# Decoder block on one core: attention values moved to head-major rows by small transfers, and divided there

## The reference

```
x = layernorm(x + selfattention(x))        # low-rank q and kv (128), rotary part, 1024 keys, softmax, @ Wo + bo
x = layernorm(x + crossattention(x, ctx))  # 154 keys, mask, softmax, @ W3.T + b3
x = layernorm(x + moe(x))                  # 8 experts, each takes its 256 best tokens, silu MLP 256-512-256
```

## Time and profile before

| what | before |
|---|---|
| time of three runs | 1958.56, 1962.59 (median), 1962.68 us |
| the profiled execution | 1959.72 us |
| its span, first to last instruction | 1957.9 us |
| mean granted PE clock | 0.907 of full speed |
| busy: PE, DVE, ACT, POOL | 85%, 58%, 46%, 22% of the span |

### The profile page before, as it was taken

The page is one execution under the profiler, slowest core; times in us unless marked ns, Lnnn a source line. Parts: engine busy times, 40 slices in busy tenths (PEclk is TensorE's granted clock), DMA queues, the critical chain, the costliest instruction groups (busy, mean ns, idle before and its releaser), DMA issues. The chain is left out here.

```text
span 1957.9 us, 32981 instructions
## 1 busy us (share of the span) xinstructions
PE 1668.1 (85%) x10632; PEld 848.3 (43%) x10632; DVE 1134.5 (58%) x1939; ACT 891.8 (46%) x1585; POOL 429.8 (22%) x547
## 2 busy tenths in 40 slices
PE   6599988798999888989998798999967844999993
PEld 3033334444332445433324354333245433888883
DVE  5577725756777256567763665677435366333424
ACT  2077773342777534347774343577833300111112
POOL 5200004302000052020001611100031001555563
PEclk9599999897999988979998899799988955999997
DMA  6700003622000044220000632200003040335446
GB/s 187 163 2 1 2 25 87 163 48 71 2 2 2 27 127 134 49 59 2 2 2 27 164 98 53 54 2 2 2 21 78 2 150 28 75 77 107 77 89 193
DMA packets 98037, 120.07 MB, mean 61 GB/s; under 512 B 17180, under 2 KB 73500, under 8 KB 97820
## 3 DMA queue, kind: packets, MB, share of 16 engines
q1 hardware_dynamic: 85468, 97.13, 18.1%
q0 software_dynamic: 12416, 20.98, 5.7%
HBM read 80.30 MB, written 40.79 MB: 62 GB/s over the span
## 5 line engine op out<-in xcount | busy, mean ns | idle before, releaser
L881 ACT ACTIVATE pT<-banks 128x512 f32<-128x512 f32 x1184 | 645.2, 596 | 254.8 <-PE banks L1492 150.0
L1034 DVE TENSOR_REDUCE nmf<-banks 128x1 f32<-128x1024 f32 x512 | 606.0, 1220 | 173.5 <-PE banks L1442 171.6
L1492 PE MATMUL banks<-qst,kst 99*128 99x512 bf16 x1024 | 344.0, 388 | 12.1 <-DVE nmf L1034 6.3
L1442 PE MATMUL banks<-kst,qst 96*128 96x512 bf16 x1024 | 327.0, 404 | 31.9 <-DMA kst<-k_parts 21.8
L1524 PE MATMUL banks<-pT,V 128*32 128x512 f32 x2048 | 273.8, 606 | 20.6 <-ACT oT L872 14.0
L1492 PEld LDWEIGHTS banks<-qst,kst 99*128 99x128 bf16 x1024 | 96.0, 97 | 307.2 <-ACT pT L881 185.8
L703 POOL CAST nmp<-nmf 128x16 bf16<-128x16 f32 x64 | 12.7, 198 | 831.4 <-DVE nmf L1034 516.6
L944 ACT ACTIVATE kst<-banks 128x512 f32<-128x512 f32 x64 | 38.2, 597 | 287.0 <-PE banks L1747 278.6
L1442 PEld LDWEIGHTS banks<-kst,qst 96*128 96x128 bf16 x1024 | 98.6, 100 | 146.4 <-DVE nmf L1034 37.3
L1029 DVE TENSOR_REDUCE nmf<-banks 128x4 f32<-128x616 f32 x128 | 99.6, 797 | 86.6 <-PE banks L1436 79.7
L1053 DVE RECIPROCAL rz<-banks 128x16 f32<-128x16 f32 x64 | 16.1, 251 | 204.5 <-PE banks L1552 203.4
(11 more groups left out here) (176 smaller groups left out, 2016.7 us busy)
## 6 DMA issues: line engine op xcount, KB each, us to landing
qst<-q_parts SPq DMA_DIRECT2D x48, 256.0 KB, 5.2
kst<-k_parts SPq DMA_DIRECT2D x48, 256.0 KB, 3.8
qst<-in_w SPq DMA_DIRECT2D x16, 512.0 KB
q_parts<-kst SPq DMA_DIRECT2D x48, 128.0 KB, 2.5
k_parts<-kst SPq DMA_DIRECT2D x48, 128.0 KB, 3.9
qx_parts<-kst SPq DMA_DIRECT2D x48, 128.0 KB, 3.1
qxs<-qx_parts SPq DMA_DIRECT2D x24, 256.0 KB, 5.0
qst<-qx_parts SPq DMA_DIRECT2D x24, 256.0 KB, 4.9
```

What stands on the lines that cost most here:

```text
L881: act.activation(pT[:, n % RING_P, :], PS[:, banks[what, n], :], ACT.Exp, scale=scale).then_inc(s_ex, 1)
L1034: dve.tensor_reduce(nmf[:, m % 2, j, t:t + 1], scores.rearrange("p a n -> p (a n)"), AX.X, ALU.max, negate=True).then_inc(s_smu, 1)
L1442: ins = pe.matmul(pair[:, half, :], qst[0:KQ, h, t * P:(t + 1) * P], kst[0:KQ, h, half * N:(half + 1) * N], start=True, stop=True)
L1492: ins = pe.matmul(ps, kst[0:KM, head, kc * P:(kc + 1) * P], qst[0:KM, head, cols], start=True, stop=True)
```

## The change

`empty` copies the bank into one of two slots `avr[:, group % 2, :]`. When it has done so, SP issues five DMAs for the group (`compact`): one takes the four rows of sums to 4 partitions of `sums` (32 x 512 when all are there: 2 x head + half), four take 16 rows of 2 KB each to the rows of the head in `xT`. In self-attention `compact(g - 2)` stands behind `load_minus_max(g)`, the last two behind `load_x(b + 1)`; in cross-attention `compact(g - 4)`, the last four behind `load_ones`. ACT waits for the transfers of group g - 2 before it fills a slot. In the junction DVE (`divided`) waits for all transfers and inverts `sums` in one instruction, 32 partitions x 512. PE (`inverses`) spreads the inverses over the rows of the heads with four float32 matmuls (32 rows of the operand `spread` of zeros and ones, 512 columns), and DVE multiplies them into `xT` with 4 instructions of 128 x 512. `output` follows, and takes a half as soon as its two multiplications are done. `o_tiles`, `turn_tokens` and the copies of the junction are gone.

The order changes with it: `latents` (b+1) stand ahead of `inverses` and `output`, `context_values` (b+1) too, on PE and on DVE; POOL's `split` of the context's keys stands ahead of the second `rsqrt`. `xTf`, `mask_i` have rooms of their own, `load_x` waits for the first st instead of the last, and ACT's wait for the mask goes. POOL makes `spread` once with a memset and four selects.

```diff
-EACH = Plan(OUT_SELF + LATENTS + INTO_CROSS + OPERANDS, OUT_CROSS + CONTEXT + ROUTING)
+EACH = Plan(LATENTS + OUT_SELF + INTO_CROSS + OPERANDS, CONTEXT + OUT_CROSS + ROUTING)
...
+            def compact(b, cross, g):
+
+                wait_apart(sp, s_ave, b * 2 * NG + (NG if cross else 0) + g + 1)
+                slot = avr[:, g % 2, :]
+                sp.dma_start(sums[TILES * g:TILES * (g + 1), :], slot[HD:P:V32, :]).then_inc(s_oc[g % 2], 16)
+                for j in range(TILES):
+                    (h, half), rows = (g * G + j // HALVES, j % HALVES), slice(V32 * j, V32 * j + HD)
+                    sp.dma_start(xT[h % 8 * HD:(h % 8 + 1) * HD, h // 8, half * N:(half + 1) * N],
+                                 slot[rows, :]).then_inc(s_oc[g % 2], 16)
...
             def self_attention(b):
                 for g in range(NG):
                     load_minus_max(b, g, qst[:, g * G:(g + 1) * G, :])
+                    if g >= 2:
+                        compact(b, False, g - 2)
...
                     load_minus_max(b, NG + g, cross_rows(g))
+                    if g >= 4:
+                        compact(b, True, g - 4)
                 if more:
                     load_ones()
+                for g in range(NG - 4, NG):
+                    compact(b, True, g)
...
-                    if n0 == 0 and k == 0:
-
-                        act.wait_ge(s_mask, b + 1 + START)
-                    act.activation(oT[:, k, :], PS[:, AV_BANK, :], ACT.Copy).then_inc(s_ave, 1)
+
+                    act.wait_ge(s_oc[k % 2], 80 * (b * NG + (NG // 2 if n0 else 0) + k // 2) + START)
+                    act.activation(avr[:, k % 2, :], PS[:, AV_BANK, :], ACT.Copy).then_inc(s_ave, 1)
...
+            def divided(at, b, name, cross):
+
+                for i in range(2):
+                    dve.wait_ge(s_oc[i], 80 * (b * NG + (NG if cross else NG // 2)) + START)
+                dve.reciprocal(sums[:, :], sums[:, :]).then_inc(s_rz, 1)
+                for n in range(4):
+                    idx, (half, c) = at.nth(name, n), divmod(n, 2)
+                    cols = slice(half * N, (half + 1) * N)
                     ready(at, idx)
...
+                    dve.tensor_tensor(xT[:, c, cols], xT[:, c, cols], PS[:, at.bank(idx), :],
+                                      ALU.mult).then_inc(s_evd, 1)
...
+            def inverses(at, b, name, cross):
+
+                pe.wait_ge(s_rz, b * 2 + (2 if cross else 1))
+                for n in range(4):
+                    half, c = divmod(n, 2)
+                    pe.matmul(item(at, at.nth(name, n)), spread[:, c, half, :], sums[:, :],
+                              start=True, stop=True).then_inc(s_item, 1)
 
             def output(at, t_name, y_name, w):
-                taken_upto(at, at.nth(t_name, 3) + 1)
                 for k in range(4):
+                    taken_upto(at, at.nth(t_name, k // 2 * 2 + 1) + 1)
...
-                o_tiles(at, "o", 0, T)
-                turn_heads(at, "o", "oT")
-                output(at, "oT", "y", wo)
                 if more:
                     latents(at, b + 1)
+                inverses(at, b, "bc", False)
+                output(at, "bc", "y", wo)
...
-                o_tiles(at, "ox", 0, T)
-                turn_heads(at, "ox", "oxT")
-                output(at, "oxT", "yx", w3)
                 if more:
                     context_values(at)
+                inverses(at, b, "bcx", True)
+                output(at, "bcx", "yx", w3)
```

More of the change, by code:

```diff
@@ L251, in decoder_block @@
         mhalf = sb("mhalf", [P, T])
-        oT = sb("oT", [P, NG, N])
-        early = oT[:, :, :].rearrange("p g n -> p (g n)")
-        mask_i = early[:, 0:T * SK].bitcast(I32).rearrange("p (t k) -> p t k", k=SK)
+        avr = sb("avr", [P, 2, N])
+        mask_i = sb("mask_i", [P, T, SK], I32)
+        sums = sb("sums", [H * HALVES, N])
+        spread = sb("spread", [H * HALVES, C, HALVES, P])
+        xTf = sb("xTf", [P, C, S])
         xT = sb("xT", [P, C, S])
@@ L410, in decoder_block @@
         s_ave = sem("values_taken")
+        s_oc = [sem(f"values_compacted{i}") for i in range(2)]
+        s_rz = sem("sums_inverted")
         s_z = sem("stats_ready")
@@ L551, in rest_of_batch @@
                     load_x(b + 1)
+                for g in range(NG - 2, NG):
+                    compact(b, False, g)
                 wait_apart(sp, s_qx[0], b * 96, s_qx[1], b * 96, s_ql[1], b * 96 + 96)
@@ L670, in _ @@
             link(pool.memset(Vr[:, :, HD:HD + 1], 1.0))
+            link(pool.memset(spread[:, :, :, :], 0.0))
+            for c in range(C):
+                for half in range(HALVES):
+                    link(pool.affine_select(out=spread[:, c, half, :], in_=spread[:, c, half, :],
+                                            compare_op=ALU.not_equal, fill=1.0, base=-H * c - half,
+                                            pattern=[[-HALVES, P // HD], [0, HD]], channel_multiplier=1))
             link(pool.memset(kxst[:, :, :], 1.0))
@@ L740, in batch @@
                     split_max(b + 1, 0, 0, SM_SELF // NG, range(1))
+                if more:
+                    split(b + 1, 8, 9)
                 rsqrt(b, 1)
                 if more:
-                    split(b + 1, 8, 9)
                     mask_bias(b + 1)
@@ L1035, in maximum, with residual_sum @@
                                               AX.X, ALU.max, negate=True).then_inc(s_smu, 1)
[L1037 to L1049, removed]
[L1050 to L1061 removed]
+            def divided(at, b, name, cross):
[5 more added lines that the diff above has]
+                    cols = slice(half * N, (half + 1) * N)
+                    ready(at, idx)
+                    dve.tensor_tensor(xT[:, c, cols], xT[:, c, cols], PS[:, at.bank(idx), :],
+                                      ALU.mult).then_inc(s_evd, 1)
+            def residual_sum(at, b, name, half, meanwhile=None):
+                if half == 0 and name == "yx":
+                    dve.wait_ge(s_xb, b * 2 + 2 + START)
+                elif half == 0:
+                    dve.wait_ge(s_x2, b * 16 + START)
+                    dve.wait_ge(s_xb, b * 2 + 1 + START)
                 for k in (2 * half, 2 * half + 1):
```

79 lines of the change are left out of this document (21 added, 58 removed).

## The result

| what | before | after |
|---|---|---|
| median, lowest and highest of 4 runs | 1960.57 (1956.58 to 1962.68) | 2041.11 (2038.14 to 2042.77) us |
| ratio, with its 95% interval | | 1.0412 [1.0388, 1.0435] |
| the profiled execution, its span | 1959.72, 1957.9 | 2042.77, 2041.0 us |
| mean granted PE clock | 0.907 | 0.886 |

Slower, as forecast, but by 80.5 us where 41 were forecast: above the range's 2021. The page of after beside the earlier trace rows: busy time of the engines, DVE's costliest group, and the new inversion.

What follows compares the result with a forecast made beforehand. PE was busy 85%, DVE 58%, but only the eight junctions were priced: self 15.2 + 5.05, cross 14.4 + 6.3, 41 us on 1959.7 gave 2001, stated as 2002 from the runs' median. Range 1978 to 2021.

Steps and rivals of the forecast that it cites:

- self term of batch 0: Self junction of batch 0: `output` starts 3.7 us later and the part behind it costs 1.15 more, 4.8 us.
- rival 3: Cross-attention: SP becomes the bound, up to 3.2 us a group delaying the maxima's rows, +50 us, 2050; chance 0.03.
- rivals 1 and 4: Junctions: 0.7 us inversion with clock kept, 1984, chance 0.16; chain hidden, 1965 or faster, chance 0.1 for both signs.
- Rival 2: Junctions: long chain, inversion of 4.3 to 7.9 us or landings of 4, +6 to +27 more, 2008 to 2029; chance 0.15.
- c: Junctions: time from the last copy to inverted sums, forecast as 8.25 us in cross and 7.9 in self batch 3.
- the prediction's formula: All junctions: added time at full clock is 5c - 13.4 us, plus 2.7 for each of five resumptions at half clock.
- At nothing: Attention stages and moved pieces: the other 7 groups' transfers and the earlier `parts` and `split` cost no time, nobody waits.
- each resumption: Junctions: PE going on after a gap of some us runs about 5.4 us at half clock, costing 2.7 us.

Runs made afterwards that it cites:

- e1: The changed kernel with POOL's mask and residual of the next batch made to wait for DVE's normalise: 2007.32 us, ratio 1.0253 to the kernel before.
- e2: The changed kernel with only POOL's residual waiting for DVE's normalise, the mask running beside it: 2020.91 us, ratio 1.032 to the kernel before.
- e7: The kernel before with one needless POOL addition of about 4.5 us behind the second `rsqrt` of each self junction: 1969.52 us, ratio 1.0092.
- e10: The changed kernel with `spread` and `sums` grown from 32 to 128 rows and nothing else: 2015.13 us, ratio 1.0316 to the kernel before.
- e11: The changed kernel with POOL waiting for normalise, needless PE matmuls during the wait for sums, and 128 rows for the inverses: 1976.63 us, ratio 1.0119.
- e3: The changed kernel with needless matmuls while PE waits for the sums, in all cross junctions and self batch 3: 2017.22 us, ratio 1.0317.
- e9: e11 plus two last-group transfers issued by ACT, inversion in two halves, and filler matmuls before the transposes behind `output`: 1949.78 us, ratio 0.9988.

## Why the prediction was right in its sign and wrong in its size

**Right.** The self term of batch 0 (+4.8 forecast, +4.8 measured: 36.72 - 31.95) and the end of `qx` behind `output` there (16.9 forecast, 16.7). That its self term came out to a tenth is partly luck: in batches 1 and 2, with the same instructions, +5.2 was forecast and +7.0 and +3.7 came. `output` 12.84 us behind the copy in self 0 (12.7). The inversion: 3.34 us against 3.1, so (3341 - 202) / 504 = 6.2 ns an element. (The estimate by the Trainium skill, VectorE: DVE Perf Modes, section "Walkthrough: the 8-slice pipeline in each mode", had been 4.3; the measurement decides.) SP's issues at 0.6 us each. The attention stages at nothing, so rival 3 has no place; rivals 1 and 4 needed a short chain, and 5.8 us to the landing with 3.34 of inversion rule both out. Rival 2 wanted an inversion of 4.3 us or more or landings of 4; the last landing was seen 1.8 us behind the end of its issue, and c is 446.86 - 437.73 = 9.1 instead of 8.25. (In the prediction's formula the constant is 13.2, not 13.4, by its own terms, which changes nothing.)

**Wrong, the step that failed.** It stands under "At nothing": "ACT's `parts` and POOL's `split` of the context come earlier, nobody waits." The step asked who waits for what is moved; it didn't ask what the move lets start. `split` gone from behind the second `rsqrt`, the mask and the residual run beside normalise. Price: logits at 17.02 instead of the forecast 8.76, 8.25 us in each of three junctions, 24.8 together. e1 takes it away (24.7 back), e2 takes away half, e7 puts it into the kernel before. This is more than half of the 45 us that the forecast lacked.

**Wrong, a term mis-sized: the clock.** The forecast gave each resumption 5.4 us at half clock, 2.7 us of cost, read off. Measured were 11.6 in cross 0: `inverses` 7.19 instead of 6.15, and `output` 9.07 to 9.92 instead of 7.17 in the cross junctions, 9.70 and 8.93 in self 1 and 3. The lengths of `output` alone add 13.3 us over all junctions. Those rows had PE resume with operands of 128 rows; here it resumes with 32. With 128 rows (e10) the forecast's 6.15 and a full-speed `output` (7.07) are what the profile shows.

**Smaller.** `output` starts 1.9 us later than forecast in cross 0: 0.75 up to the landing (one of the five issues took 1.31 us instead of 0.59), 0.24 for the inversion, 1.04 for `inverses`. Over the eight junctions later starts make some 9 us. 24.8 + 13.3 + 9 is 47; some 2 us come back behind `output`, and 45 is what the junctions show over the forecast (86 - 41).

**How the loss of 4.1% divides,** by ratios: POOL beside normalise 1.6% (after to e1), the operand of 32 rows 1.0% (after to e10), the chain at full clock 1.2% (e11). Each interval is about 0.3% wide to either side, so these are rough shares; by its rows e1's edit gives back 24.7 us, 1.3%, and the rest of its ratio lies in junctions that the edit doesn't touch. That leaves 0.3 to 0.7% for the clock behind the gap. No run measures it by itself, but e10's `inverses` are 12.7 us, 0.65%, over full clock in the five junctions where PE waits.

**Open.** That the 32 rows are a cause is shown by e10; how they act isn't. Nor is it known why they bring the clock down in some junctions and not in others: self 1 of after has `output` in 9.70, self 2 in 7.17, with the same instructions ahead; e3 has 9.85 and 7.18 for two cross junctions. And that e1's junctions are 30.7 us shorter than after's where its edit explains 24.7; the rest lies mostly in self 1 (-3.9) and cross 3 (-2.4), neither of which the edit touches, and would be the same variation; that is not shown.

## What to carry to other kernels

When an instruction is moved away, ask what was queued behind it and what that will now run beside, not only who waits for it: a short POOL piece was what kept a 4.4 us POOL instruction off DVE's normalise. Before pricing "beside", read min, median and max of each critical line, and what another engine does where the max stands: 395/406/852, with POOL's 0.77 and 0.85 beside it, already showed that DVE's instruction stands while POOL works. Where a short matmul block uses few rows and a long one follows, try the operand with all rows filled: here it gave 1%. And an exchange of transposes for a chain of transfer, inversion and spread could only pay here where the chain's latency, 12 to 13 us at full clock (e11) and still 10 to 13 with every repair (e9), is shorter than the work that it replaces, 8 to 9 us.

## What was not expected of the hardware

- Four matmuls of 32 rows went with a half clock, 1.2 GHz, in the `output` behind them in 42 of 56 junctions. Behind 5 us of full work and a gap of 1.2 us the granted clock fell while they ran (e3: `output` 9.85 us). The same with 128 rows never did (7.07 to 7.17 in 32 of 32 junctions).
- DVE's `tensor_scalar` of 128x256 stands until the POOL instruction beside it ends: 4573 ns instead of 408. An addition that reads a bank didn't: 0.41 us beside a POOL instruction of 4.41.
- A float32 reciprocal takes 6.2 ns an element: 3341 ns for 512 a partition, where the multiplication of 512 takes 0.69 us.
